# A one-core cross-attention and mixture-of-experts layer: the attention step over one pair of heads and 512 tokens

## What is computed

```python
def xattn(h, ctx, mask, Wq, Wk, Wv, Wo, q_norm_w, k_norm_w):   # 32 query heads, 8 key/value heads, head size 128
    q = (h @ Wq.T).reshape(B, 64, 32, 128).transpose(0, 2, 1, 3)
    k = (ctx @ Wk.T).reshape(B, 64, 8, 128).transpose(0, 2, 1, 3)
    v = (ctx @ Wv.T).reshape(B, 64, 8, 128).transpose(0, 2, 1, 3)
    q, k = rmsnorm(q, q_norm_w), rmsnorm(repeat(k, 4), k_norm_w)
    probs = softmax(einsum('bhqd,bhkd->bhqk', q, k) / sqrt(128) + mask)
    out = einsum('bhqk,bhkd->bhqd', probs, repeat(v, 4))
    return out.transpose(0, 2, 1, 3).reshape(B, 64, 4096) @ Wo.T
x = x + tanh(g_xattn) * xattn(layernorm(x), ctx, ...)
x = x + tanh(g_ffn) * moe(layernorm(x), ...)     # shared expert of 512, and the best 2 of 16 experts of 128
```

## Time and profile before

| | |
|---|---|
| median of 3 runs | 1478.57 us (1478.54 to 1479.4) |
| the profiled execution | 1493.04 us, its span 1491.2 us |
| TensorE busy in the span | 1443.6 us (97%) |
| VectorE, ScalarE, GpSimd busy | 856.2, 505.3, 313.4 us |
| mean granted clock of TensorE | 0.985 |

### The profile page before, as it was taken

The page is one execution under the profiler, slowest core; times in us unless marked ns, Lnnn a source line. Parts: engine busy times, 40 slices in busy tenths (PEclk is TensorE's granted clock), DMA queues, the critical chain, the costliest instruction groups (busy, mean ns, idle before and its releaser), DMA issues.

```text
span 1491.2 us, 30893 instructions
## 1 busy us (share of the span) xinstructions
PE 1443.6 (97%) x10637; PEld 1225.6 (82%) x10638; DVE 856.2 (57%) x1848; ACT 505.3 (34%) x1129; POOL 313.4 (21%) x329
## 2 busy tenths in 40 slices
PE   6999998999999999999999999999998999899986
PEld 5888887888888888888888888888887788677764
DVE  4444446565666656666565665656788651344457
ACT  4333343333333333333333333333332501222220
POOL 1222223112121121212212121121212000333352
PEclk9999999999999999999999999999999999999997
DMA  6544431111111011111111111111122234655465
GB/s 207 175 120 134 120 114 36 39 32 44 35 35 39 32 39 39 35 37 34 39 33 41 35 35 39 32 39 47 61 75 83 93 124 180 224 165 167 142 196 171
DMA packets 91524, 125.36 MB, mean 84 GB/s; under 512 B 7840, under 2 KB 56992, under 8 KB 90976
## 3 DMA queue, kind: packets, MB, share of 16 engines
q1 hardware_dynamic: 85168, 104.16, 21.7%
q0 software_dynamic: 6320, 20.71, 4.9%
HBM read 87.36 MB, written 37.49 MB: 84 GB/s over the span
## 4 chain that ended last, share of the span: by engine, by line
PE 90%; DVE 5%; issue 2%; DMA 2%; another core or an unknown queue 1%; ACT 0%; POOL 0%; SPq 0%; DVEq 0%; POOLq 0%
PE ps L503 22%; PE ps L505 21%; PE ps L504 21%; PE ps L781 5%; PE ps L569 5%; PE ps L609 4%; PE ps L797 3%; PE ps L578 2%; PE ps L595 2%; PE ps L776 1%; DVE acc L1436 1%; PE ps L550 1%; DMA acc<-in_wv 1%; DMA wgu<-in_w_gu 1%
## 5 line engine op out<-in xcount | busy, mean ns | idle before, releaser
L430 POOL TENSOR_TENSOR qr<-qv,mhalf 128x8 f32<-128x8 f32 x64 | 105.2, 1643 | 733.0 <-DVE qv L1136 733.0
L503 PE MATMUL ps<-hT,w0h 128*128 (+2 forms) x640 | 198.4, 310 | 0.9 <-DVE w0l L1069 0.9
L504 PE MATMUL ps<-hT,w0l 128*128 (+2 forms) x640 | 195.6, 306 | 0.0
L505 PE MATMUL ps<-hT,w0h 128*128 (+2 forms) x640 | 195.4, 305 | 0.0
L1121 DVE TENSOR_TENSOR acc<-ps,acc 128x512 f32 (+1 forms) x129 | 88.7, 688 | 144.1 <-PE ps L505 144.1
L945 ACT CAST ah<-ps 128x256 fp32r<-128x256 f32 x256 | 83.4, 383 | 256.5 <-PE ps L505 253.9
L1127 DVE TENSOR_TENSOR al<-ps,ah 128x256 fp32r<-128x256 f32 x256 | 96.1, 418 | 98.5 <-ACT ah L945 98.2
L503 PE MATMUL ps<-hT,w1h 128*128 (+1 forms) x512 | 147.2, 287 | 0.0
L504 PE MATMUL ps<-hT,w1l 128*128 (+1 forms) x512 | 144.7, 283 | 0.0
L505 PE MATMUL ps<-hT,w1h 128*128 (+1 forms) x512 | 144.6, 282 | 0.0
L503 PEld LDWEIGHTS ps<-hT,w0h 128*128 128x128 f32 x640 | 122.5, 191 | 7.8 <-DVE w0l L1069 1.1
(11 more groups left out here) (222 smaller groups left out, 3150.8 us busy)
## 6 DMA issues: line engine op xcount, KB each, us to landing
wraw<-in_w_att SPq DMA_DIRECT2D x64, 256.0 KB, 2.6
ybuf<-ye SPq DMA_DIRECT2D x47, 256.0 KB, 2.0
vbuf<-vo SPq DMA_DIRECT2D x16, 512.0 KB, 3.3
kbuf<-ko SPq DMA_DIRECT2D x16, 512.0 KB, 3.8
kt<-kbuf SPq DMA_DIRECT2D x64, 128.0 KB, 2.0
vt<-vbuf SPq DMA_DIRECT2D x64, 128.0 KB, 2.0
wgu<-in_w_gu SPq DMA_DIRECT2D x4, 2048.0 KB, 8.0
craw<-in_ctxT SPq DMA_DIRECT2D x9, 512.0 KB, 4.7
```

What stands on the lines that cost most here:

```text
L430: pool.tensor_tensor(qr[:], qv[:], mhalf[:, 0:8], ALU.pow).then_inc(q_rt, 1)
L503: pe.matmul(dst, l_hi, r_lo, start=first, stop=False)
L504: pe.matmul(dst, l_lo, r_hi, start=False, stop=False)
L505: return pe.matmul(dst, l_hi, r_hi, start=False, stop=last)
```

## The change

The unit of a step becomes one pair of heads over two chunks, 512 tokens. Step i = 2d + odd takes pair `odd` of the chunks 2d and 2d+1.

- `q_head` makes 12 matmuls with 512 tokens moving in place of twice 12 with 256; a step has two of them (h = 0, 1, banks 0 and 1). The second one is cut in two, and the transposes stand between its halves
- Probabilities times v need both pairs of heads of a chunk, and so two steps. `pt` doubles; `probs_v(r, part)` and the outputs of step r run in step r+1. In an odd step `probs_v(i-1, 0)` stands where it stood; in an even step `probs_v(i-1, 1)` stands before the transposes
- `scores` waits for `pT_evac` itself
- The keys of two chunks (256 KB) are loaded once for two steps. In SP's queue the order is now: `wraw` (after `w_lo`), in odd steps `kt` (after `s_done`), the tiles of x, `vt`
- Step 0 has neither `probs_v` nor outputs; the tail has two `project_out` and one `probs_v` more, and VectorE's tail the work that goes with them

Its core (the other engines' counts are shifted by one step in the same way):

```diff
-            qs = sb("qs", [P, 2, CB, 2, S], F32, a)
-            sq = sb("sq", [P, 2, CB, 2, S], F32, a)
+            qs = sb("qs", [P, 2, 2 * CB, S], F32, a)
+            sq = sb("sq", [P, 2, 2 * CB, S], F32, a)
...
-            pt = [sb(f"pt{'hl'[q]}", [P, 2, HG * S], F32R, a) for q in range(2)]
+            pt = [sb(f"pt{'hl'[q]}", [P, 4, HG * S], F32R, a) for q in range(2)]
...
-            kt = sb("kt", [P, CB, S], F32, a)
+            kt = sb("kt", [P, 2 * CB, S], F32, a)
...
+            def load_k(d):
+                sp.dma_start(kt[:].rearrange("p (c b) t -> p c (b t)", c=2),
+                             k_pair[d]).then_inc(kt_in, 16)
...
-            def next_loads(i, x_tiles=None):
-
-                sp.wait_ge(s_done, i + 1)
-                sp.dma_start(kt[:].rearrange("p b t -> p (b t)"), kbuf[i + 1]).then_inc(kt_in, 16)
-                sp.wait_ge(v_split, 2 * i + 2)
-                sp.dma_start(vt[:].rearrange("p b t -> p (b t)"), vbuf[i + 1]).then_inc(vt_in, 16)
-                if x_tiles is not None:
-                    x_tiles()
+            def next_loads(d, odd, x_tiles=()):
+
+                i = 2 * d + odd
                 sp.wait_ge(w_hi, i + 8)
                 sp.wait_ge(w_lo, i + 8)
                 sp.dma_start(wraw[:], w_att[i + NC]).then_inc(wr_in, 16)
...
+                if odd:
+                    sp.wait_ge(s_done, i + 1)
+                    load_k(d + 1)
+                for n in x_tiles:
+                    if n >= 2:
+                        sp.wait_ge(x1_done, n - 1)
+                    sp.dma_start(xt3[n % 2][:], x[n]).then_inc(x3_in[n % 2], 16)
+                sp.wait_ge(v_split, 2 * i + 2)
+                sp.dma_start(vt[:].rearrange("p b t -> p (b t)"), vbuf[i + 1]).then_inc(vt_in, 16)
...
-            def q_head(hp, h, chunk, w):
-
-                for k in range(KD):
+            def q_head(h, hp, pair, w, ks=range(KD)):
+
+                for k in ks:
                     c0 = k * 512 + (2 * hp + h) * P
-                    hc = [hT[:, bass.ds(chunk, 1), x_, k, :].rearrange("p a t -> p (a t)") for x_ in range(2)]
-                    mm = split_product(pe, PS[hp][:, h * CT:(h + 1) * CT], w[0][:, c0:c0 + P],
-                                       w[1][:, c0:c0 + P], hc[0], hc[1], k == 0, k == KD - 1)
+                    hc = [hT[:, bass.ds(2 * pair, 2), x_, k, :] for x_ in range(2)]
+                    mm = split_product(pe, PS[h][:], w[0][:, c0:c0 + P], w[1][:, c0:c0 + P], hc[0], hc[1],
+                                       k == 0, k == KD - 1)
                 return mm
...
-            def step(i, chunk_q, w_q, w_o, w_before, q_ready, o_ready):
-
-
+            def step(d, odd, pair_q, w_q, w_before, w_o, q_ready=None, o_ready=None, first=False):
+
+
+                i = 2 * d + odd
                 if q_ready is not None:
                     pe.wait_ge(w_lo, q_ready)
                 pe.wait_ge(q_sq, 2 * i + 1)
-                q_head(0, 0, chunk_q, w_q)
-                q_head(0, 1, chunk_q, w_q).then_inc(q_done, 1)
+                q_head(0, 1 - odd, pair_q, w_q).then_inc(q_done, 1)
                 pe.wait_ge(q_sq, 2 * i + 2)
-                q_head(1, 0, chunk_q, w_q)
+                q_head(1, 1 - odd, pair_q, w_q, (0, 1))
+                if not odd and not first:
+                    probs_v(i - 1, 1)
                 transpose_probs(i)
-                q_head(1, 1, chunk_q, w_q).then_inc(q_done, 1)
-                probs_v(i)
-                scores(i + 1)
+                q_head(1, 1 - odd, pair_q, w_q, (2, 3)).then_inc(q_done, 1)
+                if odd:
+                    probs_v(i - 1, 0)
+                pe.wait_ge(pT_evac, 2 * i + 2)
+                scores(d + odd, 1 - odd)
                 q_sums(i + 1)
...
+                if not first:
+                    outputs(i - 1, w_before, w_o, o_ready)
```

More of the change, by code:

```diff
@@ L574, in q_sums @@
                 pe.wait_ge(q_sq, 2 * j + 2)
-                squares = sq[:].rearrange("p a b h s -> p (a b) (h s)")
                 for r in range(4):
-                    rows = slice(32 * r, 32 * r + 32)
-                    mm = pe.matmul(PS[2][rows, 0:256], ones32[:], squares[:, :, rows], start=True, stop=True)
+                    s0 = 32 * (r % 2)
+                    mm = pe.matmul(PS[2][32 * r:32 * r + 32, 0:256], ones32[:], sq[:, r // 2, :, s0:s0 + 32],
+                                   start=True, stop=True)
                 mm.then_inc(ss_done, 1)
@@ L642, in _, with group @@
+            scores(0, 0)
             pe.wait_ge(acc_zero, 4)
             q_sums(0)
-            def group(i0, p, last=False):
-                step(i0, 1, W[p], W[p], W[1 - p], None, i0 + 8)
-                with pe.Fori(0, NC - 2) as t:
-                    step(i0 + 1 + t, t + 2, W[p], W[p], W[p], None, i0 + 8)
+            def group(d0, p, first=False, last=False):
+                i0 = 2 * d0
+                step(d0, 0, 0, W[p], W[1 - p], W[1 - p], first=first)
+                step(d0, 1, 1, W[p], W[1 - p], W[p], o_ready=i0 + 8)
+                with pe.Fori(0, NC // 2 - 2) as t:
+                    step(d0 + 1 + t, 0, t + 1, W[p], W[p], W[p])
+                    step(d0 + 1 + t, 1, t + 2, W[p], W[p], W[p])
+                step(d0 + NC // 2 - 1, 0, NC // 2 - 1, W[p], W[p], W[p])
@@ L955, in act_step, with act_group @@
                 squares(0, i + 1)
[L956 removed]
+                probs_hi(i, odd)
                 q_out(1, i + 1)
                 squares(1, i + 1)
[L959 to L960 removed]
+                if not first:
+                    a_hi_tile(i - 1, 0)
+                    a_hi_tile(i - 1, 1)
                 split_slice(i, w, sl)
                 exps(i + 1)
+            def act_group(d0, p, t0=0):
+                with act.Fori(t0, NC // 2) as t:
+                    for odd in range(2):
+                        act_step(d0 + t, odd, W[1 - p], 2 * t + odd)
+            act_step(0, 0, W[1], 0, first=True)
+            act_step(0, 1, W[1], 1)
+            act_group(0, 0, 1)
             with act.Fori(0, KVH // 2 - 1) as gg:
                 for p in range(2):
[L966 to L968 removed]
+                    act_group(NC // 2 + NC * gg + NC // 2 * p, 1 - p)
             act.wait_ge(g_in, 16)
@@ L1182, in residual, with dve_step @@
                 dve.bn_stats(st, row).then_inc(st_done, 1)
-            def dve_step(i, w, sl, tile, tile_before, complete=(None, None)):
-                probs_lo(i)
+            def dve_step(d, odd, w, sl, tile_before, tile, complete=(None, None), first=False):
+                i = 2 * d + odd
+                probs_lo(i, odd)
                 if complete[0] is not None:
                     residual(complete[0], 1)
-                a_rest(i, 0)
+                if not first:
+                    a_rest(i - 1, 0)
                 if complete[1] is not None:
@@ L1193, in while_root, with while_exp @@
                 def while_root():
-                    add_out(2 * i + 1, 1, tile_before)
-                    a_rest(i, 1)
-                softmax(i + 1, while_root, lambda: add_out(2 * i + 2, 0, tile))
+                    if not first:
+                        add_out(2 * i - 1, 1, tile_before)
+                        a_rest(i - 1, 1)
+                def while_exp():
+                    if not first:
+                        add_out(2 * i, 0, tile)
+                softmax(i + 1, while_root, while_exp)
                 slice_lo(i, w, sl)
```

204 lines of the change are left out of this document (105 added, 99 removed).

## The result

| | before | after |
|---|---|---|
| time, median (lowest to highest), us | 1478.89 (1478.54 to 1479.4), 4 runs | 1544.14 (1538.76 to 1545.91), 4 runs |
| profiled execution: time / span, us | 1493.0 / 1491.2 | 1538.76 / 1536.9 |
| TensorE busy, share of the span | 97% | 93% |
| start of the scores of step 1 to those of step 63, us | 894.1 | 948.4 |
| start of the scores of step 63 to the first gate and up product, us | 43.0 | 51.2 |

The changed kernel is slower by 65 us: ratio 1.043, 95% interval 1.041 to 1.045. The forecast was 1529 us with the range 1506 to 1556; the range holds the time, the middle of it was 15 us too low.

The account below looks back on a forecast made before the run. TensorE was taken as the bound, nine tenths of the chain that ended last. Keys 44.6 + pairs 31 x 0.05 + ends 4.6 = 50.8 us, added to 1478.6, gave 1529 us, range 1506 to 1556.

Parts of the forecast that it names:

- keys: Odd steps: kt, queued behind wraw, lands late and the scores wait 1.44 us, 31 times: 44.6 us (26 to 69).
- the rest of the steps: Pairs of steps apart from the keys: saved matmul overhead goes to exposed copy and evacuation wait, +0.05 us a pair.
- head: Step 0 has no output products: bare softmax chain gains 2.1 us, lower clock takes about 1.7 back.
- tail: After the last step: two output products and one probs_v more on TensorE, VectorE's sums and residuals: 5.0 us (0 to 6.3).
- The gain of the bare softmax chain and the cost of the lower clock: Step 0 to step 1: chain without output products gains 2.1 us; the stop lowers TensorE's clock, about 1.7 us back.
- Fewer, longer matmuls: q's projection: 512-column matmuls at 0.227 us replace pairs at 0.120, saving 0.32 us a step, 20 us in all.
- the odd step without its wait: Odd step without its loads: scores could start at about 9.60 us of the step, 0.30 earlier than before.
- The even step: Scores directly behind q wait for ScalarE's copy of q: start at 10.25 us, 0.35 later than before (0.25 to 0.5).
- The keys cost nothing: Rival: kt lands within 1.36 us of issue, odd scores never wait, leaving 1.6 + 4.6: 1485 us; chance 0.07.
- faster, 1463: Rival: kt in time and copy of q faster, so the 20 us come whole and only ends cost: 1463 us; chance 0.07.
- the clock goes down in each pair: Rival: stops in each pair drop TensorE to 1.2 GHz, 1.7 us for each of 31: 1582 us; chance 0.05.
- What I cost at nothing: Loads of v, x tiles behind kt in odd steps, GpSimd's inverse root and doubled pt: no added time.

Follow-up runs that it names:

- experiment 1: Changed kernel with kt in odd steps issued right after the previous step's scores, ahead of the wait for slice_lo and of wraw: 1514.15 us, ratio 1.015.
- the repeat: The changed kernel itself, unaltered, timed again beside the kernel before in the second comparison: 1540.64 us, ratio 1.042.
- experiments 1 to 3: Changed kernel, kt ahead of the slice_lo wait and wraw: 1514.15 us; ahead of wraw only: 1531.86; kernel before, 128 KB kt behind wraw: 1558.24.
- Experiment 5: Kernel before with half of project_out(1), 6 of 12 matmuls, moved between the last matmul of q and probs_v: 1481.86 us, ratio 1.002.
- experiment 4: Changed kernel with kt issued early and, in every step but the first, half of project_out(1) moved right behind q: 1490.89 us, ratio 0.998.
- Experiment 6: Changed kernel with early kt, half of project_out(1) behind q, VectorE's tail reordered and four h2 stores ahead of the last x tile: 1476.35 us, ratio 0.998.
- experiment 3: Kernel before with only its 128 KB load of kt moved behind wraw in SP's queue, in every step: 1558.24 us, ratio 1.044.

## Why the prediction was right, and where it was not

| term of the sum | predicted, us | measured, us | from |
|---|---|---|---|
| keys | 44.6 (26 to 69) | 40.6 | steps, after less experiment 1 |
| the rest of the steps | +1.6 | +13.0 | steps, experiment 1 less before (13.7), less the 0.7 of step 1 |
| head | -0.4 | 0.0 | start of the scores of step 1, 235.24 less 235.93, and the 0.7 of step 1 |
| tail | +5.0 (0 to 6.3) | +8.2 | 51.2 less 43.0 |
| sum | 50.8 | 61.8 | |

The head is too small to be told: in the trace of the repeat the scores of step 1 start at 236.83, 1.6 us later than in the first trace of the same kernel. The gain of the bare softmax chain and the cost of the lower clock, which the prediction set against each other, both lie in step 1. Its transposes do wait for the softmax (2.61 us), and the granted clock from 245 to 249 us is 0.61.

*The sign and the main term.* The keys were right in cause, place and size. Issue of `wraw` at 7.59 (7.58 predicted), of `kt` at 8.18 (8.24), landing 2.8 (2.8), scores at 10.95 (11.04). The order in the queue costs it, as experiments 1 to 3 show from three sides. The keys cost 4 us less than forecast, a term well inside its bounds. The chain of reasoning that found it is worth repeating: follow the moved DMA back to what its new neighbours in the queue wait for, and forward to its first user.

*Fewer, longer matmuls.* q's matmuls are 0.227 apart in the new kernel (505.81 to 506.49 above is three of them), and the odd step without its wait is 0.28 shorter than before (14.14 in experiment 1), 0.30 predicted. By the 2.5 ns a matmul of the Trainium skill, "TensorE: Matmul & The Clock Gate", section "Back-to-back issue gap", 24 matmuls less would have saved only 0.06 us a step. The measured step decides for the 13 ns.

*The even step is the term that failed.* Predicted: scores at 10.25 of the step, with bounds 10.15 to 10.4. Measured: 10.58, outside the bounds. The 0.33 us consist of four pieces of 0.08 to 0.09. `probs_v` starts 0.32 behind the last q matmul and not 0.23 (506.49 to 506.81). From `probs_v` to the transposes it takes 0.90 and not 0.82 (506.81 to 507.71). From the transposes to the end of q it takes 1.87 and not 1.79 (507.71 to 509.36 + 0.22); they themselves are slower behind `probs_v` than behind q, 0.41 to the next matmul (507.71 to 508.12) where the odd step has 0.36 (521.81 to 522.17). And the scores start 0.92 behind that end, not 0.83 as in the earlier trace rows.

The first three stand where one kind of matmul follows another. In the odd step the kinds follow each other as before, and it came out right; in the even step they follow in a new order, and I carried neither the gap ahead of `probs_v` nor the one behind it over to it. The row was there: the earlier trace rows shows 0.21 where 0.12 was due, and I booked it as time lost at that place. Experiment 5 shows that it was no wait.

The fourth piece is another matter: in the earlier trace rows as here the scores follow q and wait for the copy of q. It is the same in the changed kernel before its first step:

```profile
219.68 0.39 PE L514 MATMUL ps<-hT,w0h 128*128 128x512 f32 x1
...
220.82 1.15 PE L578 MATMUL ps<-kt,qs 128*64 128x64 f32 x32 [0.76 <-ACT qs L939]
```

From 219.68 + 0.23 to 220.82 it is 0.91. ScalarE starts the copy no later behind the end of q than before; the scores start 0.72 us behind its start (509.78 to 510.50), and 0.64 before the change (220.84 to 221.48). Where these 0.08 us come from stays open; VectorE's evacuation, for which the scores now wait as well, had ended at 509.55.

Over 31 pairs 0.33 us are 10 of the 11 us by which that term was off; most of the rest is the odd step, 0.28 shorter and not 0.30.

*So the rivals that rest on free keys were mis-sized too.* "The keys cost nothing" was set at 1485 us, 6 above the kernel before. Experiment 1 is just that case and stands 21 us above it. And "faster, 1463" would have needed the filling of experiment 4 besides, which brings only 10.7 us in the steps and loses 8 of them again in the tail (51.1 against 43.0).

*The tail.* Predicted 5.0, at most 6.3; measured 8.2. The bound was TensorE's own extra work: two output products and one `probs_v`, 6.3 us. The prediction names VectorE's extra work but adds nothing for it to the upper end, and TensorE waits for it later. The longest wait of TensorE in the tail, released by the rest part of `hT`, grew from 1.84 to 4.83 us (the kernel before, then the changed one):

```profile
1157.10 0.63 PE L680 MATMUL ps<-ident,h 128*128 128x128 f32 x4 [1.84 <-DVE hT L1257]
...
1218.91 3.54 PE L705 MATMUL ps<-ident,h 128*128 128x128 f32 x16 [4.83 <-DVE hT L1297]
```

From the scores of step 63 to the first transposes of the normalised tokens TensorE takes 5.2 us more than before (1183.63 to 1212.17 against 1130.00 to 1153.35), and this wait 3.0 more: both engines' additions fell one behind the other and not side by side. A bound from one engine's work is no upper bound where a second engine, full as in the earlier trace rows, has extra work too. Experiment 6 takes 2.1 us of it back with the same work on both engines.

*The clock.* The rival "the clock goes down in each pair" did not come: in spite of a stop of 1.24 us in every pair the granted clock over the steps of the changed kernel (third last entry of the row, columns as in the earlier trace rows) is 1.00.

```profile
240.00:1180.00 940.00, 875.90 (x6359) 688.04 (x6358) 561.89 (x1245) 324.11 (x798) 169.36 (x184) 1.00 0.12 37
```

*What I cost at nothing.* The loads of v and the tiles of x made no new wait of TensorE in the steps. The tiles of x are free only because they stand behind the keys; experiment 3 shows what they cost in front of them. That the gap between the profiled execution and the median (14.5 us) lies outside the steps fits the traces: with and without the waits in the down projection, the stretch behind the attention differs by as much.

## What to carry to other kernels

When an edit moves a DMA, its new place in the issuing queue is a dependency on everything that the neighbours in front wait for; write down the time at which it can be issued, add the landing time of its size behind those neighbours, and compare with its first use. Here that alone was 41 of 54 us in the loop, and giving the load its old place in the queue undid it. Larger steps that save issue time pay only if what they no longer hide (here a copy of 0.8 us) is covered by other work of the bound engine; moving half of an independent product there turned a loss of 13.7 us in the steps into a gain of 10.7.

## What the runs showed of the hardware

- Some changes from one kind of matmul to another cost TensorE about 0.09 us even where nothing is waited for: from 128 rows to the 64 rows of `probs_v` 0.32 in place of 0.23 us (510.05 to 510.37 in experiment 5), from `probs_v` to the scores 0.21 in place of 0.12 (511.06 to 511.27). From q to the transposes there is no such gap (521.58 to 521.81).
- A load of 256 KB issued 0.6 us behind another of 256 KB on the same queue lands only 0.1 us later than with nothing in front of it (2.8 against 2.7 us). One of 128 KB, issued 0.43 us behind such a load, lands 0.5 us later than alone (2.5 against 2.0). So half the size saved 0.7 us of the landing alone, and 0.3 behind a neighbour.
- Late in the kernel, in code outside any loop, TensorE waits in some executions with nothing recorded that holds it: 5.9 us in the 35 us from 1440 in the profile of the kernel before. Five of ten profiles have 6 to 12 us of it, five have none or 0.2, and kernels with and without the change are found on both sides. The same kernel's median differed by 13 us between two comparisons. Differences of that size are not to be put down to an edit without a run beside it on the same chip.
